# Two cross-attention layers: f16 context parts, a context load of 12 keys per partition, and layer 0's preparation matmuls in a scores bank

## The reference, cut to what matters

```python
# layer 0: differential attention, 32 sub-heads of 4
q, k, v = query @ Wq.T, key_ @ Wk.T, value @ Wv.T      # key_ = value = ctx_1024, (32, 1500, 128)
attn = softmax(q1 @ k1.T) @ v - lam * (softmax(q2 @ k2.T) @ v)     # then RMS norm per head
x = x + tanh(g) * (attn @ Wp.T + bp)
x = x + tanh(g) * experts(layernorm(x))
# layer 1: masked attention, 16 heads of 8, over the same context
q, k, v = query @ Wq.T + bq, key @ Wk.T + bk, value @ Wv.T + bv
scores = where(mask, lowest, q @ k.T / sqrt(8))
x = x + tanh(g) * (softmax(scores) @ v @ Wo.T + bo)
x = x + tanh(g) * experts(layernorm(x))
```

## Time and profile before

| | us |
|---|---|
| median of 3 runs | 2521.49 |
| lowest, highest | 2520.28, 2526.41 |
| profiled execution | 2527.04 |
| its span, first to last instruction | 2525.3 |
| L0's steady batch, L948 to L948 | 38.79 |
| L1's steady batch, L948 to L948 | 23.90 |
| L0's attention, first T to the last A drained | 38.3 to 1360.3 |
| L1's attention | 1528 to about 2350 |

### The profile page before, as it was taken

The page is one execution under the profiler, slowest core; times in us unless marked ns, Lnnn a source line. Parts: engine busy times, 40 slices in busy tenths (PEclk is TensorE's granted clock), DMA queues, the critical chain, the costliest instruction groups (busy, mean ns, idle before and its releaser), DMA issues. The chain is left out here.

```text
span 2525.3 us, 64926 instructions
## 1 busy us (share of the span) xinstructions
PE 2334.8 (92%) x26296; PEld 1302.1 (52%) x26296; DVE 1707.5 (68%) x3732; ACT 1486.3 (59%) x2101; POOL 1057.9 (42%) x1150
## 2 busy tenths in 40 slices
PE   4799999999999999999996976999999999999798
PEld 3344444444444444444444763566655666666576
DVE  2478788778787787787872653666656666666444
ACT  2156767767777667677774432566656666666422
POOL 4213333333233333333323347456655665663232
PEclk8579999999999999999997986899999999999799
DMA  3524534434445345344411006667665765762100
GB/s 101 106 57 81 107 88 82 108 78 96 99 80 103 90 80 110 77 95 99 83 32 49 23 28 141 113 125 139 129 112 126 130 130 123 139 132 47 51 1 15
DMA packets 157410, 227.67 MB, mean 90 GB/s; under 512 B 46052, under 2 KB 106596, under 8 KB 156612
## 3 DMA queue, kind: packets, MB, share of 16 engines
q1 hardware_dynamic: 157124, 223.67, 42.2%
HBM read 146.77 MB, written 76.48 MB: 88 GB/s over the span
## 5 line engine op out<-in xcount | busy, mean ns | idle before, releaser
L943 ACT ACTIVATE probs<-score_ps 125x896 f32<-125x896 f32 x1152 | 1013.7, 916 | 402.4 <-PE score_ps L850 401.5
L1001 DVE TENSOR_REDUCE max_part<-max_ps 112x1 f32<-112x500 f32 x1023 | 665.1, 672 | 155.1 <-PE max_ps L829 84.2
L866 PE MATMUL acc_ps<-probs,vext 125*32 125x224 f32 (+1 forms) x12288 | 678.6, 316 | 2.4 <-issue 1.4
L829 PE MATMUL max_ps<-kstack,qstack 48*112 48x500 f16 x1534 | 510.3, 406 | 23.2 <-ACT vext L928 11.9
L998 DVE CUSTOM_DVE_ANT_0 kstack<-max_ps,kstack 112x500 f32<-112x500 f32 x511 | 335.0, 675 | 156.3 <-PE max_ps L829 88.0
L1001 DVE TENSOR_REDUCE max_part<-spare_ps 112x1 f32<-112x500 f32 x513 | 344.6, 672 | 131.7 <-PE max_ps L829 119.2
L720 POOL CAST khl<-kstack 128x500 f16<-128x500 f32 x192 | 115.0, 599 | 709.5 <-ACT kstack L926 521.4
L866 PEld LDWEIGHTS acc_ps<-probs,vext 125*32 125x32 f32 x12288 | 258.3, 109 | 269.5 <-issue 262.3
L850 PE MATMUL score_ps<-qstack,kstack 50*125 50x224 f16 (+1 forms) x6144 | 388.6, 244 | 1.7 <-ACT probs L943 1.7
L850 PEld LDWEIGHTS score_ps<-qstack,kstack 50*125 50x125 f16 x6144 | 305.5, 135 | 151.0 <-issue 120.9
L829 PE MATMUL spare_ps<-kstack,qstack 48*112 48x500 f16 x770 | 311.6, 405 | 16.0 <-ACT vext L928 6.2
(11 more groups left out here) (184 smaller groups left out, 2547.7 us busy)
## 6 DMA issues: line engine op xcount, KB each, us to landing
kstack<-k_parts SPq DMA_DIRECT2D x384, 187.5 KB, 6.4
k_parts<-khl SPq DMA_DIRECT2D x128, 375.0 KB, 5.5
ctx_f<-in_ctx SPq DMA_DIRECT2D x32, 750.0 KB
context_parts<-ctx_f SPq DMA_DIRECT2D x32, 750.0 KB, 4.7
ctx_f<-context_parts SPq DMA_DIRECT2D x32, 750.0 KB, 4.3
mask_in<-in_mask SPq DMA_DIRECT2D x128, 82.0 KB
qrows<-q_parts SPq DMA_DIRECT2D x384, 7.0 KB, 7.3
qstack<-max_rows SPq DMA_DIRECT2D x384, 0.9 KB
```

The costliest lines, as they stand in the source:

```text
L829: nc.tensor.matmul(room(("P", n, p))[0:PIECE, 0:TK], qstack[n % SLOTS][rows, c, PIECE * i:PIECE * (i + 1)], kstack[n % SLOTS][rows, c, TK ...
L866: last = nc.tensor.matmul(acc_ps[32 * j:32 * j + 32, TT * S * i:TT * S * (i + 1)].rearrange("p (s c) -> p s c", s=S), vext[n % SLOTS][:, t ...
L943: nc.scalar.activation(probs[t % 2][:, 896 * h:896 * h + 896].rearrange("k (b c) -> k b c", b=2), score_ps[(t * H + h) % 2][0:KT, :, 0:448 ...
L1001: nc.vector.reduce_max(best, scores, AX.X).then_inc(s_red, 1)
```

## The change

It does these things:

1. The context, `Wk` and `Wv` are held as f16 pairs, high and low part (`w_parts`, scaled by 64). K and V become sums of three f16 products, high·high and the two mixed ones: K three matmuls of 500 columns, V twelve of 128 columns. V's drain takes the 64 back out.
2. ACT drains T into an f32 buffer of its own (`context_f`, in the free part of `kstack0`); POOL splits it (`split_context`, six new instructions for a batch of L0: two for each third). For the first three batches DVE does it. Both parts are stored to `context_parts`, 6000 B per row as before, and L1 loads them.
3. L0's context is loaded with the 12 keys 12p to 12p+11 on partition p, one HBM run of 6144 B. Chunk t then has the keys 12p+t. L1's two mask conversions read the mask with a step of 12 bytes to get the same order.
4. In L0 the place-1 uses leave the three rooms. They go into the first bank of the half whose exponential the step takes first. PE waits for that exponential ahead of the use. Which half is first alternates from step to step, and the half that held the use comes second in the next step, after the drain. The first half of a step now waits for all exponentials of the step before. `where` of L0 is set anew: T at steps 0, 2, 4, F at 1, 3, K at 5, 8, 10, V at 6, 9, 11, M stays at 7.
5. `max_rows` is ordered so that `fill_m` needs four DMAs in both layers (before eight in L0). SP issues the next context load ahead of the context's store, as soon as T is drained, and both now stand ahead of `fill_m`.

```diff
@@ setup, VectorE: for each layer i @@
-                    link(nc.vector.tensor_scalar(small[f"WkT{i}"][:, :], small[f"WkT{i}"][:, :], QK_UP, None, ALU.mult))
-                link(nc.vector.tensor_copy(wk_order[:, :].rearrange("p (r h x) -> p r h x", r=2, h=2), halves_first(small["WkT0"][:, :])))
+                    for w in range(2):
...
+                        link(nc.vector.tensor_scalar(weight, weight, QK_UP, None, ALU.mult))
...
+                        link(nc.vector.tensor_copy(high, weight))
+                        link(nc.vector.tensor_tensor(low, weight, high, ALU.subtract))
@@ load_context @@
-                     T["a"]["ctx"][n:n + 1, :, :].rearrange("b (t p) d -> (b p) t d", p=KT)).then_inc(loaded[0], 16)
+                     T["a"]["ctx"][n:n + 1, :, :].rearrange("b (p t) d -> (b p) t d", p=KT)).then_inc(loaded[0], 16)
@@ attend @@
-        where = {("V", 0): (0, 1), ("F", 0): (1, 1), ("F", 1): (2, 1), ("V", 1): (3, 1), ("T", 0): (4, 1), ("V", 2): (5, 1),
...
+        where = {("T", 0): (0, 1), ("F", 0): (1, 1), ("T", 1): (2, 1), ("F", 1): (3, 1), ("T", 2): (4, 1), ("K", 0): (5, 1),
...
-            order += searched(n, t, 0) + at_step(n, t, 1) + searched(n, t, 1) + at_step(n, t, 2)
+            middle, last = at_step(n, t, 1), at_step(n, t, 2)
...
+            if H == 2:
+                in_scores.update({user: n * NKT + t for user in middle})
+                middle = []
+            order += searched(n, t, 0) + middle + searched(n, t, 1) + last
...
+        return (0, 1) if step % 2 == 0 or H == 1 else (1, 0)
...
+        if user in in_scores:
+            return score_ps[halves_of(in_scores[user])[0]][:, 0, :]
@@ POOL @@
-                    nc.gpsimd.tensor_scalar(mask_f[n % SLOTS][0:HALF + SQ, :], mask_in[0:HALF + SQ, :], -BIG, None, ALU.mult).then_inc(s_big, 1)
+                    nc.gpsimd.tensor_scalar(by_chunk(mask_f[n % SLOTS][0:HALF + SQ, :]), turned_keys(mask_in[0:HALF + SQ, :]),
+                                            -BIG, None, ALU.mult).then_inc(s_big, 1)
...
+            def split_context(n, i):
+                k = slice(TK * i, TK * i + TK)
+                pool.wait_ge(s_ctxT, NTHIRD * n + i + 1)
...
+                nc.gpsimd.tensor_copy(ctxT[n % 2][:, 0, k], context_f[:, k]).then_inc(s_cp, 1)
+                pool.wait_ge(s_cp, high_part(n, i))
+                nc.gpsimd.tensor_tensor(ctxT[n % 2][:, 1, k], context_f[:, k], ctxT[n % 2][:, 0, k], ALU.subtract).then_inc(s_cp, 1)
@@ PE: use, scores @@
+                if user in in_scores:
+                    pe.wait_ge(s_exp, in_scores[user] * H + 1)
...
-                    nc.tensor.matmul(spare_ps[:, 0:TK], Wk[:, :], ctxT[n % len(ctxT)][:, TK * i:TK * i + TK],
-                                     start=True, stop=True).then_inc(s_ready, 1)
+                        pe.wait_ge(s_cp, low_part(n, i))
+                    for k, (w, x) in enumerate(((0, 0), (1, 0), (0, 1))):
+                        last = nc.tensor.matmul(spare_ps[:, 0:TK], Wk[w], ctxT[n % 2][:, x, TK * i:TK * i + TK],
+                                                start=k == 0, stop=k == 2)
...
+                        for k, (x, w) in enumerate(((0, 0), (0, 1), (1, 0))):
+                            last = nc.tensor.matmul(spare_ps[0:KT, D * t:D * t + D], ctxT[n % 2][:, x, c:c + KT], Wv[w],
+                                                    start=k == 0, stop=k == 2)
...
-                at_least(pe, s_exp, number - 1)
...
+                elif place == 0:
+                    at_least(pe, s_exp, number)
+                else:
+                    at_least(pe, s_exp, number - 2)
+                    for user in in_scores:
+                        if in_scores[user] == step - 1:
+                            pe.wait_ge(*drained(user))
```

More of the change, by code:

```diff
@@ L463, in attend @@
     ctx_in = ctx_f[0:KT, 1, :].rearrange("p (t d) -> p t d", t=NKT)
-    ctxT = [ctx_f[:, i, 0:SK] for i in range(1 + L.masked)]
     qrows, mask_in, out_sb = T["qrows"], T["mask_in"], T["out_sb"]
@@ L476, in attend @@
     key_f = T["kstack"][1][:, K_WORDS + SK:K_WORDS + 3 * SK].bitcast(F32)
+    ctxT = [context_parts(T, 0), context_parts(T, 1) if L.masked else
+            T["kstack"][2][:, K_WORDS:K_WORDS + 2 * SK].rearrange("p (a k) -> p a k", a=2)]
+    context_f = T["kstack"][0][:, K_WORDS:K_WORDS + 2 * SK].bitcast(F32)
     qstack = [T["qstack"][i][:, 0:PAIRS * GC].rearrange("p (c q) -> p c q", c=PAIRS) for i in range(SLOTS)]
-    Wk, Wv = (small["WkT1"] if L.masked else T["wk_order"]), small[f"WvT{layer}"]
+    Wk, Wv = ([T["w_parts"][:, layer, w, part, :] for part in range(2)] for w in range(2))
     S = L.heads // VH
@@ L581, in piece @@
         r, third, c, i = p % 2, p // 2 % NTHIRD, p // (2 * NTHIRD) % PAIRS, p // (2 * NTHIRD * PAIRS)
-        return r, third, c, i, (i * 2 + r) * PAIRS + c
+        return r, third, c, i, (r * PAIRS + c) * L.parts + i
     with nc.Block() as block:
@@ L633, in fill_m @@
                 sp.wait_ge(s_mr, n + 1)
+                half = L.tiles // 2
                 for part in range(2):
@@ L636, in fill_m @@
                         row = HALF * r + KROWS + part
-                        for i in range(L.parts):
-                            u = (i * 2 + r) * PAIRS
-                            sp.dma_start(qstack[n % SLOTS][row:row + 1, :, PIECE * i:PIECE * (i + 1)],
-                                         max_rows[u:u + PAIRS, part, 0:PIECE]).then_inc(s_mrow[n % SLOTS], 16)
+                        sp.dma_start(qstack[n % SLOTS][row:row + 1, :, :].rearrange("a c q -> a (c q)"),
+                                     max_rows[half * r:half * (r + 1), part, 0:PIECE]).then_inc(s_mrow[n % SLOTS], 16)
             def next_context(n):
@@ L677, in _ @@
                         next_context(n + 4)
+                if n + 3 < B and not L.masked:
+                    next_context(n + 4)
+                    store_context(n + 3)
                 if n + 1 < B:
@@ L764, in _ @@
                     prepare(n + 2)
+                if L is L0 and n + 3 < B:
+                    split_context(n + 3, 0)
+                    split_context(n + 3, 1)
                 if n:
                     finish(n)
+                if L is L0 and n + 3 < B:
+                    split_context(n + 3, 2)
                 if n + 3 < B:
@@ L1005, in reduce_piece @@
                                             negate=True).then_inc(s_neg, 1)
-            for user in first_preps:
-                drain(user)
+            for n in range(3 if L is L0 else 0):
+                for i in range(NTHIRD):
+                    k = slice(TK * i, TK * i + TK)
+                    dve.wait_ge(s_ctxT, NTHIRD * n + i + 1)
+                    if n == 2 and i == 0:
+                        dve.wait_ge(s_v, NTHIRD)
+                        dve.wait_ge(s_cst, 16)
+                    nc.vector.tensor_copy(ctxT[n % 2][:, 0, k], context_f[:, k]).then_inc(s_cp, 1)
+                    dve.wait_ge(s_cp, high_part(n, i))
+                    nc.vector.tensor_tensor(ctxT[n % 2][:, 1, k], context_f[:, k], ctxT[n % 2][:, 0, k], ALU.subtract).then_inc(s_cp, 1)
             for p in range(L.pieces):
```

97 lines of the change are left out of this document (61 added, 36 removed).

## The result

| | before | after |
|---|---|---|
| median, us | 2523.95 (4 runs) | 2426.89 (4 runs) |
| lowest, highest | 2520.28, 2526.77 | 2416.64, 2430.21 |
| profiled execution, its span | 2527.04, 2525.3 | 2430.21, 2428.4 |
| first output copy of L0 | 180.6 | 165.7 |
| L0, first to last output copy | 1168.2 | 1120.9 |

The ratio of the times is 0.9609, 95% interval 0.9577 to 0.9642: 4% faster. The predicted 2420 is 7 us (0.3%) too low. The span lost 96.9 us, in three places: the start 14.9, L0 47.3, L1 35.8; the stretch between the layers took 1.1 more.

The account below looks back on a forecast made before the run. PE's program was taken to set the pace in both layers. L0 -51, L1 -44, start -8 and setup +2 made -101: 2426 us profiled, 2420 on the median's footing; range 2392 to 2482.

Parts of the forecast that it names:

- f16 products: K and V on PE: K falls to 0.77 us, saving 0.27; V to 0.83, saving 0.24.
- Rival (a): V on PE: weight loads don't hide; at 81 ns V saves nothing, +52 us, whole 2472; chance 0.11.
- The forecast of 36.8: L0's steady batch: from 38.79 to about 36.8 us, 1.9 to 2.0 less.
- The wait of 0.16: L0's middle uses: PE waits 0.16 us for the step's first exponential in nine steps, 1.45 us a batch.
- rival (c): L0's middle uses: the wait for the exponential grows to, say, 0.4 us, +60, whole 2480; chance 0.07.
- Around M: L0's M step: about 0.45 us net of rooms' waits removed, though DVE's drain still pushes its reductions.
- The stall of step 1: L0, step 1: PE's wait for ACT, which copies the output before draining, stays and grows by 0.2 us.
- The tail: L0's last batches: first scores wait for both exponentials before, 2.2 us a step for 1.73; 17 steps cost +7.
- L1: L1's batches: K and V shorter by 1.53 us a batch, 23.90 to 22.4; 29 batches, -44 us.
- a loss of clock: PE's clock, granted in full in all three stretches: given no price and little chance.
- GpSimd: L1's mask conversion with a 12-byte step: 5 to 6 us each, up to 7.1 free, so cost zero.
- The rest: Start and setup: context loads asked for earlier, in longer runs, save 8 us (bounds 0 and 15); DVE setup +2.3.

Follow-up runs that it names:

- e11_less_traffic: Changed kernel with L1's context loads cut to 128 of 3000 elements a partition from the third batch on; excess of the first 28 batches 14.0 us.
- e3_short_runs: Changed kernel with L0's context load back in single rows and L1's mask converted in its own key order; first output copy at 170.7 us.
- e5_tail: Changed kernel with the halves of the scores changing places only after a step that held a use; 2419.1 us, ratio 0.9564.
- e1_rooms: Changed kernel with L0's middle uses back in the three rooms and halves in fixed order; 2429.7 us in one run, 2433.9 (ratio 0.9666) when timed again.
- e8_mask_twice: Changed kernel with GpSimd converting each piece of L1's mask twice; whole 2634 us, L1 batch 30.4 us (median).

## Why the prediction held, point by point

**f16 products.** K 0.74 and V 0.84 against 0.77 and 0.83. Inside V one matmul starts 58 ns after the other (median of the distances in 77 V's of L0), which is the 57 ns taken from the earlier trace rows, now at full height of the array; the change of weights at both ends is the other 0.14 of 0.837. Rival (a) is out. The Trainium skill, page "TensorE: Matmul & The Clock Gate", section "Back-to-back issue gap", gives about 81 ns for a sustained pair. That doesn't hold for these pairs; the measurement decides.

**L0.** The forecast of 36.8 became 36.90, but two of its parts were off in opposite senses: f16 gave 1.36 alone and not 1.53, the banks on top of it 0.53 and not 0.4. The six uses did get 3 x 0.30 + 3 x 0.23 = 1.59 shorter, and L1's batch by just that; why 0.23 of it is missing in L0 with the three rooms isn't shown. The wait of 0.16 ahead of the use came as computed, so rival (c) is out. In the steady batches PE never waited for POOL's split of the context. Around M I counted 0.45 as removed; 0.25 behind M and 0.28 in the next step stay, since DVE's drain of M still delays its reductions. The stall of step 1 was seen and forecast to grow by 0.2; with 0.90 of wait ahead of the scores it is L0's largest, and the prediction took it as given where it was an order on ACT that could be turned round (0.82 a batch).

**The tail** was forecast at 2.2 a step and +7: 2.23, and +6.8 (2.0 and 4.8 in the last two batches). In the sum for L0, -51 was forecast and -47.3 measured between the copies. The 28 steady batches gave 53.5 where 55 was forecast, and of the 3 for the first and third last batch only 0.6 shows there; the first batch ends with the first copy and so lies in the start's part.

**L1** is where a term was mis-sized: -44 forecast, -35.8 in the profiled run. The steady batch fell by 1.58, as said (1.53), which over 28 batches is 44. But batches that are longer than the steady one took some of it back: in the first 28 of a trace their excess is 15.2 us in the changed kernel and 12.1 before, and the last three take 58.3 and 52.8. On the average of more traces it is 17.0 and 11.4, 53.8 and 51.4. Over nine traces of kernels with the new L1 (in one of them the mask is read in order) the stretch takes 691.7 to 701.4, on average 695.6, and in three with the old L1 734.1, 735.3 and 726.9, on average 732.1. So 36.5 is the gain, and about 8 us come back. The prediction multiplied a steady batch by their number and didn't look at the others.

The traces show what happens in the long ones. PE stands still before an instruction with no releaser. In the records of the DMA queue that brings instructions in pieces of 16 KB (82 in the 609 us above; 211 of them are about 64 B for each of PE's 54512 loads and matmuls, so I take them for PE's), the pieces come every 7.5 us on average in the new L1. In 13 traces PE stood still like this for over 1 us sixty times in L1, and each time the same two things hold: it went on 1.2 to 1.8 us after such a piece had landed, and that piece had started 12 to 15 us after the one before. In the changed kernel only six distances in L1 are that long; five end in such a gap, the sixth in a stop of 1.0 us that the profile puts down to ACT. So PE's instructions come late there; no run moved a piece, and what makes one late stays open. Less data traffic doesn't change it.

Nor do the gaps move from trace to trace, as I had written ahead of `e11_less_traffic`. Seven of these traces have the f16 parts and the uses in the banks. Of their 35 gaps all but one stand before the same matmuls, counted from the program's start: the 18854th, 19233rd, 19612th, 25046th and 25425th, or one batch (379 matmuls) ahead of the first or the fourth. The three with f16 parts and the uses in the rooms have all 14 at five other places (the 15744th, 16123rd, 21557th, 21936th and 22315th). PE by time at the 19612th in `e3_short_runs` and `e5_tail`:

```profile
1867.06 0.38 PE L930 MATMUL score_ps<-qstack,kstack 50*125 50x112 f16 x6 [2.79 <-issue]
1852.58 0.38 PE L935 MATMUL score_ps<-qstack,kstack 50*125 50x112 f16 x6 [2.58 <-issue]
```

A gap costs more than its length, since in many cases PE's clock falls to half behind it. One in the changed kernel, then the same window of time in `e1_rooms`, where no gap stands near:

```profile
2202.08 0.59 PE L946 MATMUL acc_ps<-probs,vext 125*32 125x112 f32 x16 [1.84 <-issue]
...
2204.00:2220.00 16.00, 16.00 (x194) 9.91 (x198) 9.50 (x32) 7.09 (x10) 0.00 (x0) 0.50 0.01 2
2204.00:2220.00 16.00, 15.83 (x312) 10.20 (x312) 13.55 (x45) 11.09 (x16) 4.14 (x4) 1.00 0.17 23
```

That batch took 27.30 us, and 20.25 in `e1_rooms`: 1.84 of standing still, the rest at half clock (0.50). In L1 as a whole half clock was granted for 27 us in the changed kernel and for 10 before, on average 17 in the nine traces and 6 in the three. The prediction gave a loss of clock no price, since it was "granted in full in all three stretches"; the second row has 0.99 there.

**GpSimd.** The conversion took 4.76 us and not 5 to 6:

```profile
L760 POOL TENSOR_SCALAR kstack<-mask_in 112x1500 bf16<-112x1500 uint8 x32 | 151.7, 4740 | 2.6
L757 POOL TENSOR_SCALAR kstack<-mask_in 120x1500 f16<-120x1500 uint8 x32 | 152.3, 4758 | 0.0
```

That is 19% above the 3994 ns of the earlier trace rows, and `e3_short_runs`, which reads the mask in order, has 3993 again. The half more per element that the Trainium skill, page "GPSIMD Engine Reference", section "Performance pitfalls for Q7 kernels", gives for a step over 8 bytes is too much for this instruction. The cost for the time is nil, as said; by `e8_mask_twice` it would begin at 4.75 + 6.4/2 = 7.9 us a conversion (7.1 was forecast).

**The rest.** -8 and +2 were forecast, -14.9 came. The +2 is right: PE's first instruction starts 2.6 later (20.5 and 23.1). So the part forecast at 8 was 17.5, above its upper bound of 15. 10.1 of the 14.9 are the earlier first exponential; the remainder goes with the moment of full clock, which the prediction gave no price and which moves the first copy by 4 us from trace to trace. That the total is only 7 us off is in part luck: the excess of 9 here and the shortfall of 8 in L1 nearly cancel, and the good total hides both.

## What to carry to other kernels

Before a buffer is moved so that a wait disappears, ask which waits its new place adds in the stages where there is nothing to put into it: here the banks cost in the tail about as much as they gave without the f16 parts, and nearly half of it with them, until the alternation was tied to their use. An engine that stands in order before an operand that isn't ready, with a ready one behind it, is worth an exchange of two instructions: 0.82 us a batch for no work removed, seen as idle time of the engine ahead of its copy and not of the one that pays. And a steady batch times their number is no stage: sum the real distances of the trace first. A short stop of PE is to be priced with the clock behind it, 2.5 us of waiting with 5.6 of half clock in `e8_mask_twice`.

## What wasn't expected of the hardware

Ahead of L0's first copy PE's clock fell to half for the last time at 78 to 93 us from the start (before: inside a wait of 6.9 us for the context; in the changed kernel: at the first searches, with waits of 0.17 us between them), and stayed there until 135 to 153 us; kernels with the same start came to full clock up to 13 us apart, worth 4 us. GpSimd's conversion of bytes with a step of 12 costs 4.76 us for 3.99. PE's gaps without a releaser, mostly 1 to 3 us each, appear in every trace of L1 that was looked at, of before and after. They stand at the same instructions for the same program of PE, each behind a piece of instructions that started 12 us or more after the one before, and half clock was seen behind a stop of only 1.7 us.
